# Second attention: where a group's last values and its second copy of sums stand

## The reference

```python
qkv = hidden_states @ w_attn + b_attn
scores = jnp.einsum('bqhd,bkhd->bhqk', q, k) * SCALE
bias = slopes[:, None, None] * rel[None, :, :]
scores = jnp.where(causal[None, None], scores + bias[None], -jnp.inf)
attn = jax.nn.softmax(scores, axis=-1)
out = jnp.einsum('bhqk,bkhd->bqhd', attn, v).reshape(B, S, HIDDEN)
return out @ w_proj + b_proj
```

## Time and profile before

| | us |
|---|---|
| three runs | 1717.48, 1720.41, 1723.44 (median 1720.41) |
| the profiled execution, its own time | 1718.02 |
| its span in the trace | 1716.1 |
| second attention, first exponential to the end of the last copy | 1144.17 to 1611.39 |
| one of its inner groups | 29.17 to 29.22 |

### The profile page before, as it was taken

The page is one execution under the profiler, slowest core; times in us unless marked ns, Lnnn a source line. Parts: engine busy times, 40 slices in busy tenths (PEclk is TensorE's granted clock), DMA queues, the critical chain, the costliest instruction groups (busy, mean ns, idle before and its releaser), DMA issues. The chain is left out here.

```text
span 1716.1 us, 32400 instructions
## 1 busy us (share of the span) xinstructions
PE 1631.0 (95%) x12784; PEld 832.8 (49%) x12784; DVE 1388.8 (81%) x2959; ACT 963.4 (56%) x1095; POOL 213.0 (12%) x272
## 2 busy tenths in 40 slices
PE   6998999999999999999999999999999999999899
PEld 3554333333333333333344777654545454544487
DVE  3777799999999999999448364568898988889486
ACT  3433288888888888887811111126666666666420
POOL 3332200000000000000022021010031210000233
PEclk9999699999999999999999999989999999999999
DMA  7766334334334333331140433665463736353231
GB/s 218 227 175 212 83 58 82 63 65 65 63 63 66 67 61 59 58 61 61 57 161 25 147 98 104 219 160 102 73 101 64 110 62 111 62 96 81 72 117 74
DMA packets 116799, 167.55 MB, mean 98 GB/s; under 512 B 20772, under 2 KB 58036, under 8 KB 116532
## 3 DMA queue, kind: packets, MB, share of 16 engines
q1 hardware_dynamic: 115176, 160.99, 41.4%
q0 software_dynamic: 1472, 4.49, 1.3%
HBM read 100.41 MB, written 64.50 MB: 96 GB/s over the span
## 5 line engine op out<-in xcount | busy, mean ns | idle before, releaser
L358 DVE TENSOR_REDUCE mxp<-ps_m 128x1 f32<-128x512 f32 x1280 | 801.1, 685 | 45.5 <-PE ps_m L324 39.9
L708 ACT ACTIVATE a_p<-a_ps_s 128x1024 f32<-128x1024 f32 x512 | 521.0, 1026 | 150.3 <-PE a_ps_s L616 132.7
L708 ACT ACTIVATE b_p<-b_ps_s 128x1024 f32<-128x1024 f32 (+1 forms) x320 | 294.6, 938 | 158.7 <-PE b_ps_s L616 155.2
L355 DVE CUSTOM_DVE_ANT_0 ps_m<-ps_m,b_masks 128x128 f32<-128x128 f32 (+3 forms) x512 | 240.1, 517 | 41.3 <-PE ps_m L324 36.7
L324 PE MATMUL ps_m<-slot_qk 62*128 62x512 f32 (+3 forms) x624 | 230.8, 451 | 11.9 <-DVE mxp L358 9.0
L324 PE MATMUL ps_m<-a_slot_qk 62*128 62x512 f32 x640 | 239.3, 451 | 0.9 <-DVE mxp L358 0.9
L616 PE MATMUL a_ps_s<-a_slot_qk 64*128 64x512 f32 x640 | 232.7, 444 | 0.0
L645 PE MATMUL a_ps_o<-a_p,a_slot_v 128*32 128x256 f32 (+1 forms) x2400 | 203.4, 405 | 0.0
L616 PEld LDWEIGHTS a_ps_s<-a_slot_qk 64*128 64x128 f32 x640 | 96.2, 185 | 138.1 <-issue 114.9
L281 POOL CAST cparts<-negm 128x16 fp32r<-128x16 f32 x64 | 12.6, 197 | 1084.5 <-DVE negm L364 1084.5
L616 PE MATMUL a_ps_s<-slot_qk 64*128 64x512 f32 x384 | 136.5, 455 | 0.2
(11 more groups left out here) (217 smaller groups left out, 2382.7 us busy)
## 6 DMA issues: line engine op xcount, KB each, us to landing
va_tokens<-w_o SPq DMA_DIRECT2D x16, 512.0 KB, 2.8
ka_parts<-pa_parts SPq DMA_DIRECT2D x16, 512.0 KB, 3.0
qa_parts<-pa_parts SPq DMA_DIRECT2D x32, 256.0 KB, 3.8
kb_parts<-slot_memory SPq DMA_DIRECT2D x16, 512.0 KB, 3.5
qb_parts<-slot_memory SPq DMA_DIRECT2D x32, 256.0 KB, 3.3
vb_tokens<-w_proj SPq DMA_DIRECT2D x16, 512.0 KB, 2.7
a_slot_qk<-qa_parts SPq DMA_DIRECT2D x60, 128.0 KB, 4.1
a_slot_qk<-ka_parts SPq DMA_DIRECT2D x48, 128.0 KB, 6.6
```

Of the source, the lines that this page charges most:

```text
L355: dve.tensor_tensor_reduce(from_, from_, mask_of_query[:, CHUNK - keys:], 1.0, LOWEST, ALU.add, ALU.max, accum_out=to).then_inc(piece_take ...
L358: dve.tensor_reduce(to, from_, AX.X, ALU.max).then_inc(piece_taken, 1)
L708: act.activation(p_sb[:, (2 * u + pair) % NP, :, off:CHUNK], ps_s[:, 2 * pair:2 * pair + 2, off:CHUNK], ACT.Exp, scale=scale).then_inc(exp ...
```

## The change

In the second attention the values of a group's last unit (u9) now stand behind the scores of the next group's u0, as in the first attention, and the copy of their sums stands behind the two exponentials of that u0. Only the last group keeps both where they were. No instruction is added or taken away; the first attention stays as it is.

```diff
                     if u:
                         values(s, s % SLOTS, u - 1, part)
-                    elif s and not causal:
+                    elif s:
                         values(s - 1, (s - 1) % SLOTS, NU - 1, part)
...
-                    if causal or s == NG - 1:
+                    if s == NG - 1:
                         values(s, j, NU - 1, 0)
                         values(s, j, NU - 1, 1)
...
-                        if u == 0 and s and not causal:
+                        if u == 0 and s:
                             copy_out(s - 1, 1)
-                    if causal or s == NG - 1:
+                    if s == NG - 1:
                         copy_out(s, 1)
```

## The result

The changed kernel takes 1748.85 us (median of 4 runs, 1745.29 to 1753.27) against 1721.93 before: 1.0152 times, with a 95% interval of 1.0133 to 1.0172. The forecast was 1738, slower by 18 us, with a range to 1747; the loss is 27 us, and the time lies just above the range. The direction and the place are as forecast, the size is not.

A forecast was written before the change was run, and what follows sets the result against it. PE was taken to set the pace, DVE close behind. Waits at u3 (11.3), long issues (3.6) and the last two boundaries (1.5 + 1.5) sum to 17.9 us slower: forecast 1738 us, case bounds 1731 to 1745, stated range 1728 to 1747.

The forecast's parts named there:

- The wait taken away: At a group boundary, PE's wait for the last exponential ahead of u9's values goes: 0.15 us.
- u0, u1 and the copy: After E (end of a group's last exponential): u1 0.14 us later, copy ends 2.74 later at E + 4.31, gain 0.06.
- The chain behind the copy: Copy's end through SP's stores and maxima loads to u3's scores: 5.13 us, making PE 0.87 us late at 13 boundaries.
- Long issues: At three of 13 boundaries L545's four issues on SP take about 3 us, not 1.83: 1.2 more each, 3.6 in all.
- The sum of the delays: Over all 15 boundaries: 11.3 for waits at u3, 3.6 for long issues, 1.5 + 1.5 for the last two: 17.9 us.
- boundary 13: After group 13 DVE's reciprocals set u0 in both kernels; u3 starts at 1566.7 instead of 1565.2: cost 1.5 us.
- boundary 14: After group 14 u3 already waits 1.04 us for rows; cost 2.3 with a long issue, 0.9 without, 1.5 taken.
- the clock: Rival: PE falls to 1.2 GHz in the new pauses, 6.4 us per stretch, 96 us over 15 groups: 1834 us; chance 0.02.
- the paragraph on issuing and landing: SP's issuing is 3.76 of 5.13 us from copy to scores; were engine bandwidth the limit, the change costs nothing (1717).
- the rows landing in time: Rival: u3's maxima arrive before PE needs them, gain 15 x 0.06 = 0.9 us: 1719.5, no measurable change; chance 0.09.
- the gain by DVE's idle time: Rival: PE profits by DVE's 0.65 us idle at each boundary, 9.8 us in all: 1710.7; chance 0.04.
- a long issue at every boundary: Rival: SP's line meets other transfers at every boundary, 13 x 2.1 + 1.5 + 2.3 = 31 us: 1751; chance 0.05.

The follow-up runs named there:

- SP's new order: Changed kernel with SP issuing the two DMAs of u3's maxima ahead of the previous group's stores, second attention only: 1722.7 us, 0.9997 times before.
- the change again: The changed kernel run once more with no edit, for its spread: 1751.71 us, 1.0169 times before.
- values alone: Changed kernel with the copy put back ahead of u0's exponentials on ACT, so only u9's values are moved: 1756.08 us, 1.0225 times before.
- late rows: Kernel before, with five more small stores in each of SP's stores of the second attention, delaying u3's maxima: 1754.0 us, 1.0203 times before.
- early values: Changed kernel with SP's new order, u9's values right behind the scores of u0's first pair, copy between u0's exponentials: 1723.6 us, 1.0002 times before.
- copy alone: Kernel before with only the copy moved behind u0's two exponentials, u9's values left at their group's end: 1762.77 us, 1.0227 times before.

## Why the prediction was wrong in size

**The wait taken away** was 0.15 us, PE's own. In the profile after, PE goes from the values of u8 into u0 without it, and the gain is lost again to DVE's backlog and the copy, as worked out. With nothing late (SP's new order) groups take about 0.17 us less than before; 0.06 had been forecast.

**u0, u1 and the copy.** Forecast: u9's values at E + 2.49, copy ended at E + 4.31, u0's values at 4.38. Measured 2.51, 4.13 and 4.27. Two steps are off: DVE takes the first piece at E + 0.70 instead of 0.78, and so u0's second exponential starts at 2.62 instead of 2.71; and the copy starts 0.10 us before that exponential ends, where I had 0.02.

**The chain behind the copy.** Forecast 5.13 us from the copy's end to u3; measured 9.24 - 4.13 = 5.11. u3 in quiet groups: 9.44 forecast, 9.24 measured, so 0.67 us late instead of 0.87.

**Long issues.** Three had been kept among thirteen, at 1.2 us each. Four came (0, 2, 9, 11), 0.9 to 1.5 us beyond the quiet ones, and two more slightly long.

**The sum of the delays** of u3 was forecast as 17.9 us; the trace has 17.9, but the match to the tenth is luck. The 13 waits of 0.87 us (11.3) came to 8.7, the long issues, priced at 3.6, came to 5.4, boundary 13 was 2.0 instead of 1.5 and boundary 14 was 1.8 instead of 1.5.

**The step that failed** is the clock. I took it as a rival of its own with a chance of 0.02, all or nothing, priced at a fall in every group. As the pause of 1.04 us before had not lowered it, I let that row stand for all pauses, though my own sum had pauses twice as long at the boundaries with a long issue. It did fall there: behind u3's pauses of 1.70 to 2.33 us, for 3.4 to 13.7 us each, and what came behind u3 cost 12.8 us in the profiled execution and 9.9 in that of the change again. It belonged into the forecast as a term on the long issues. Putting work in the pause takes that term away, and reversing SP's order takes away both.

**Boundary 13** failed in the same way. I had let DVE set u0 in both kernels and looked at the time of u0's second scores alone, which is indeed the same (E + 3.38, before 3.41). PE's pause ahead of them grew from 1.06 to 1.76 us, and the clock fell behind it too. This pause wasn't priced, and it stays with SP's new order.

The two parts add up to 30.7 us in the profile and to 28.2 in the second one; between the medians there are 26.9 and, for the change again, 29.0. With the delays at 18 us in both profiles, the clock's part in a usual execution is some 9 to 11 us, an estimate (26.9 and 29.0 less 18). The forecast of 1738 had 0 for it.

The rule of the Trainium skill (TensorE: Matmul & The Clock Gate, Part 1), that the lower level is the default and activity holds the higher one, agrees in direction with these runs: the clock stayed up over 2 us of products and often fell over 2 us of idling. The stretch that I had priced at 6.4 us was near for the worst case (4.9 us behind group 0). In the paragraph on issuing and landing the 1717 should be 1720, the median before.

The other rivals: the rows landing in time, the gain by DVE's idle time, and a long issue at every boundary did not come.

## What to carry to other kernels

Before an instruction is delayed, follow what is queued behind its waiter on the in-order DMA issuer: here the stores of a copy stood ahead of two small DMAs with a deadline, and turning the two around was worth the whole loss. A new wait on TensorE can cost more than its length, by the clock behind it, so price the longest of the new pauses and not their mean. Moving a wait off an engine gains little (0.17 us a group here) when the next shared resource, here three banks and DVE's backlog, holds it at nearly the same point. And what is moved away may have filled a wait elsewhere, as the values had at the reciprocals.

## What the runs showed of the hardware

- Over all profiles together (without boundary 13), the 36 pauses ahead of u3 of 0.75 to 1.21 us were never followed by the lower clock, the 21 of 1.40 to 1.99 us were 12 times, and the 15 of 2.00 to 3.27 us were 13 times. The shortest with a fall was 1.43 us, the longest without 2.52.
- The place counts as well. Thirteen pauses of 1.64 us in u1 (values alone) brought no fall in the profiled execution. In u0 behind group 13 the clock fell in six of the seven profiles with a pause of 1.75 us (in that of values alone only behind a second pause, in u1), and in three of the five with one of 1.02 to 1.07 us (late rows, early values, and copy alone, where a second one of 0.77 us followed), though such short ones never did it ahead of u3. The length alone doesn't decide; what else does stays open.
- Behind a pause ahead of u3 the lower level lasts 3.4 to 13.7 us, in some cases from within the pause on and at the latest from 2.2 us behind its end, though PE works again at once. It differs between executions of one kernel at the same place (boundary 11: 10.2 and 3.4 us).
- SP's four issues of L545 take 1.83 us mostly and up to 3.38 in the change, at the same boundaries in both its executions and in the one with SP's new order (up to 3.10); with products in the pause they came at others (3.18 and 3.39 us at 5 and 7). What lengthens them wasn't tried.
